# A graph network with two nucleus searches: one VectorE pass fewer in each search, logits placed between products, ScalarE passes reordered, three repair depths

## What is computed

```python
def _adj_from_feats(Xa, W1, W2, W3):
    logits = (Xa @ W1) @ W2 @ (Xa @ W3).T
    idx = argsort(-logits); vals = take(logits, idx)
    csum = cumsum(softmax(vals))
    k_i = sum(csum < 0.9) + 1          # keep the k_i largest of each row
    masked = where(rank < k_i, logits, -inf)
    return softmax(masked, axis=1)

h = relu(layernorm(x));  x = x + (A @ (h @ W + b)) / deg
h = relu(layernorm(x));  S = adj + I
Xf = Xb = Xa = h;  Z = 0
for s in range(2):
    A  = _adj_from_feats(Xa, W1, W2, W3)
    Xf = Rf @ Xf;  Xb = Rb @ Xb;  Xa = A @ Xa     # Rf, Rb: S over its row / column sums
    Z += Xf @ U1[s] + Xb @ U2[s] + Xa @ U3[s]
out = x + layernorm(h + Z) * gamma + beta
```

## Time and profile before

| | us |
|---|---|
| median of 3 runs | 2577.81 (2575.78 to 2578.23) |
| the profiled execution | 2577.75, of which the span of the trace 2576.0 |
| first step, from the first tile's last pass to the last tile's | 414.9 to 1294.3 |
| second step, the same | 1396.9 to 2514.2 |

### The profile page before, as it was taken

One profiled execution on the slowest core, in us unless ns is written; L12 is line 12 of the kernel. 1 busy time (PEld: TensorE's weight loads), 2 busy tenths in 40 slices (PEclk: granted clock), 3 DMA queues, 4 the chain that ended last, 5 costly groups with the idle time before them and its releaser, 6 DMA issues. The chain is left out here.

```text
span 2576.0 us, 33332 instructions
## 1 busy us (share of the span) xinstructions
PE 2014.6 (78%) x9898; PEld 1339.5 (52%) x9898; DVE 2227.2 (86%) x6888; ACT 1680.0 (65%) x1780; POOL 962.6 (37%) x1282
## 2 busy tenths in 40 slices
PE   2999465888888888888855887888888788888883
PEld 1555223566556665556633555555655555565552
DVE  6777658899889988889849999999999999999996
ACT  4334156788778877788636776777677677767730
POOL 1000042444434444344414354444535444453524
PEclk9999787999999999999976888888888888888896
DMA  6777210111111110111042000101010010101013
GB/s 226 286 284 271 92 44 17 47 45 36 41 43 47 47 45 31 42 47 46 32 156 80 19 19 19 38 19 38 19 38 19 22 35 19 37 20 37 18 61 121
DMA packets 65717, 167.54 MB, mean 65 GB/s; under 512 B 7037, under 2 KB 45307, under 8 KB 61947
## 3 DMA queue, kind: packets, MB, share of 16 engines
q1 hardware_dynamic: 65530, 165.43, 18.6%
HBM read 117.95 MB, written 47.45 MB: 64 GB/s over the span
## 5 line engine op out<-in xcount | busy, mean ns | idle before, releaser
L1348 PE MATMUL banks<-xa,pt 128*128 128x256 f32 x2704 | 660.2, 399 | 84.7 <-ACT pt L917 84.7
L893 ACT ACTIVATE junk_a<-pb_all,minus_t 128x3327 f16<-128x3327 f32 x151 | 463.5, 3069 | 261.5 <-POOLq L823 261.4
L1348 PEld LDWEIGHTS banks<-xa,pt 128*128 128x128 f32 x2704 | 527.8, 201 | 177.7 <-ACT pt L917 106.1
L1392 PE MATMUL banks<-region,at 128*128 128x512 f16 x2028 | 468.0, 392 | 0.0
L898 ACT ACTIVATE junk_a<-pb_all,minus_t 128x3327 f16<-128x3327 f32 x151 | 463.2, 3068 | 2.8
L1312 PE MATMUL banks<-keys,qs 64*128 64x512 f32 (+1 forms) x832 | 217.4, 642 | 221.8 <-DVE pb_all L1210 182.0
L808 POOL TENSOR_SCALAR over<-over,points 128x1 f32<-128x1 f32 x151 | 57.4, 380 | 821.7 <-ACT junk_a L898 821.6
L917 ACT ACTIVATE pt<-banks 128x896 f32<-128x896 f32 x208 | 178.0, 857 | 240.4 <-PE banks L1340 240.4
L1392 PEld LDWEIGHTS banks<-region,at 128*128 128x128 f16 x2028 | 205.8, 102 | 245.3 <-issue 28.7
L1312 PEld LDWEIGHTS banks<-keys,qs 64*128 64x128 f32 x832 | 83.6, 222 | 360.8 <-DVE pb_all L1210 264.5
L1210 DVE TENSOR_SCALAR_CACHE_REDUCE pb_all<-banks 128x1024 f32<-128x1024 f32 x260 | 208.9, 848 | 62.1 <-PE banks L1312 59.9
(11 more groups left out here) (225 smaller groups left out, 3309.2 us busy)
## 6 DMA issues: line engine op xcount, KB each, us to landing
at<-adjT_d SPq DMA_DIRECT2D x52, 832.0 KB, 4.9
region<-in_adj_dram SPq DMA_DIRECT2D x25, 1663.5 KB, 8.0
adjT_d<-at SPq DMA_DIRECT2D x26, 832.0 KB, 3.9
fb_d<-fb_sb SPq DMA_DIRECT2D x26, 256.0 KB, 2.0
region<-fb_d SPq DMA_DIRECT2D x2, 3328.0 KB, 19.2
y_d<-y_sb SPq DMA_DIRECT2D x50, 128.0 KB, 1.7
x_d<-pb_all SPq DMA_DIRECT2D x1, 3328.0 KB, 10.4
qs<-q_d SPq DMA_DIRECT2D x104, 32.0 KB, 4.2
```

Source lines behind the costliest of these rows:

```text
L893: nc.scalar.activation(junk_a[:, 0:w], pb[u][:, 0:w], ACT.Relu, scale=sign, bias=t, accum_out=over[u][:, 0:1])\
L1348: last = nc.tensor.matmul(bank[4][:, 0:D], pt[sl][:, t * P:(t + 1) * P], xa[:, t0 + t, :], start=(t0 + t == 0), stop=(t0 + t == T - 1))
L1392: last = nc.tensor.matmul(bank[5 + n][:, :], at[i.slot][:, t, :], mov, start=(t == 0), stop=(t == T - 1))
```

## The change

- Constants: the first step's search has one bisection fewer on DVE (BISECTIONS 5 to 4) and sorts 24 values, not 32; the second step's has a third rough level on ACT and POOL (ROUGH 2 to 3), one verifying pass fewer (VERIFIED 2 to 1) and sorts 40 values, not 64. The cut is now interpolated in both steps, with an aim of its own.
- In the second step DVE subtracts the whole of `below`; POOL's half and the semaphores `below_late` and `kept_late` are gone.
- PE makes the first two logits chunks of tile m ahead of the third and fourth product, and only the rest behind them.
- ACT's passes stand in a table STEPS: two copies come ahead of the first pass of tile j, the last pass stands behind the `zt` copies. In the second step the passes of tile m's first and second rough level stand as before around the copies of `sx`, with the second in the middle of them, and a third level ends the body, ahead of the next body's first copy.
- In the first step POOL makes `fb` in place of ACT, behind its levels.
- A repair has three depths (4, 24, all rounds), and PE counts flags three times a tile.

```diff
-    ROUGH = (0, 2)
-    BISECTIONS = (5, 3)
+    ROUGH = (0, 3)
+    BISECTIONS = (4, 3)
     ACT_BISECTIONS = (3, 3)
-    EARLY_BISECTIONS = (0, 2)
-    AIM = (12.0, 12.0)
-    VERIFIED = (0, 2)
+    EARLY_BISECTIONS = (0, 3)
+    AIM = (6.0, 16.0)
+    CUT_AIM = (6.0, 24.0)
+    VERIFIED = (0, 1)
     SEGMENTS = (8, 16)
-    SORTED = (32, 64)
+    SORTED = (24, 40)
     WSUB = (N + 1) // 4
-    MARGIN = 0.65
+    MARGIN = 0.45
...
-    LATE_SEGMENTS = SEGMENTS[1] // 2
-    LATE = LATE_SEGMENTS * ((N + 1) // SEGMENTS[1])
-    FEW_ROUNDS = 8
+    FEW_ROUNDS = 4
+    MORE_ROUNDS = 24
     ALL_ROUNDS = -(-N // 8)
-    LOOKS = 2
+    LOOKS = 3
...
-                        pool.wait_ge(S2("fb_hi")[k.slot], 3 * (k.use + 1))
+                        pool.wait_ge(S2("xfb")[k.slot], 2 * (k.use + 1))
+                        pool.wait_ge(S2("fb_stored")[1 - k.slot], 16 * (k + 1).use)
+                        ch.add(nc.gpsimd.tensor_copy(fb_sb[:, 0:D], xf_sb[k.slot][:, :]))
+                        ch.link(nc.gpsimd.tensor_scalar(xk_sb[:, :], xb_sb[k.slot][:, :], kappa[:, :], None, ALU.mult))
+                        ch.link(nc.gpsimd.tensor_copy(fb_sb[:, 2 * D:3 * D], xk_sb[:, :]))
                         nc.gpsimd.tensor_tensor(fb_sb[:, D:2 * D], xf_sb[k.slot][:, :], fb_sb[:, 0:D], ALU.subtract)\
                             .then_inc(S2("fb_lo")[k.slot], 1)
                         nc.gpsimd.tensor_tensor(fb_sb[:, 3 * D:4 * D], xk_sb[:, :], fb_sb[:, 2 * D:3 * D], ALU.subtract)\
                             .then_inc(S2("fb_lo")[k.slot], 1)
-                    if not first and i.inside(T):
-                        pool.wait_ge(S("below_late"), i.t + 1)
-                        late = pb[i.third][:, LATE:N]
-                        nc.gpsimd.tensor_tensor(late, late, below[:, LATE:N], ALU.subtract).then_inc(S("kept_late"), 1)
                     if not first:
                         level(m, 1)
+                        level(m, 2)
...
+                STEPS = ((), (0,), (1,), (2, 3), (4,), (5,)) if first else ((), (6,), (7,), (8, 9), (10,), (11,))
...
-                        if (0 if first else 1) <= c < NT - 1 and j.inside(T):
-                            sums(j, 2 * EARLY + c - (0 if first else 1))
-                    if j.inside(T):
-                        for n in range(3, 4) if first else range(6, 8):
-                            sums(j, n)
+                        if j.inside(T):
+                            for n in STEPS[c]:
+                                sums(j, n)
...
-                        for n in range(4, 6) if first else range(8, 10):
+                        for n in STEPS[NT]:
                             sums(j, n)
-                    if m.inside(T):
-                        exponentials(m)
...
+                    if j.inside(T):
+                        for n in STEPS[NT + 1]:
+                            sums(j, n)
+                    if m.inside(T):
+                        exponentials(m)
...
-                    if first and k.inside(T):
-
-                        fb = fb_sb
-                        act.wait_ge(S2("xfb")[k.slot], 2 * (k.use + 1))
-                        act.wait_ge(S2("fb_stored")[1 - k.slot], 16 * (k + 1).use)
-                        nc.scalar.activation(fb[:, 0:D], xf_sb[k.slot][:, :], ACT.Copy).then_inc(S2("fb_hi")[k.slot], 1)
-                        act.wait_ge(S2("fb_lo")[1 - k.slot], 2 * (k + 1).use)
-                        nc.scalar.activation(xk_sb[:, :], xb_sb[k.slot][:, :], ACT.Copy, scale=kappa[:, :]).then_inc(S2("fb_hi")[k.slot], 1)
-                        act.wait_ge(S2("fb_hi")[k.slot], 3 * k.use + 2)
-                        nc.scalar.activation(fb[:, 2 * D:3 * D], xk_sb[:, :], ACT.Copy).then_inc(S2("fb_hi")[k.slot], 1)
+                                if n == 0 and m.inside(T):
+                                    for q in range(2, 4):
+                                        sums(m, q)
+                    elif not first and m.inside(T):
+                        for q in range(2, 4):
+                            sums(m, q)
                     if not first and m.inside(T):
-                        for n in range(2, 4):
+                        for n in range(4, 6):
...
-                    cut = hi_t
-                    if not VERIFIED[s]:
-                        towards(cur[:, 0:1])
-                        cut = cur[:, 0:1]
+                    towards(cur[:, 0:1], CUT_AIM[s])
+                    cut = cur[:, 0:1]
...
-                        for g in [*range(LATE_SEGMENTS, G), *range(LATE_SEGMENTS)]:
+                        for g in range(G):
                             d = below[:, g * W8:(g + 1) * W8]
-                            ins = nc.vector.match_replace(d, rank[:, 8 * g:8 * g + 8], d, 0.0)
-                            if g == G - 1:
-                                ins.then_inc(S("below_late"), 1)
-                            elif g < LATE_SEGMENTS:
-                                ch.add(ins)
+                            ch.add(nc.vector.match_replace(d, rank[:, 8 * g:8 * g + 8], d, 0.0))
                         answer(i, 1)
                         ch.all_done()
-                        ch.add(nc.vector.tensor_tensor(p[:, 0:LATE], p[:, 0:LATE], below[:, 0:LATE], ALU.subtract))
+                        ch.add(nc.vector.tensor_tensor(p, p, below[:, 0:N], ALU.subtract))
...
-                            with dve.Fori(0, ALL_ROUNDS) as g:
-                                a_round(Chain(dve, "step_settle_3", base=TAKE * ALL_ROUNDS * i.n + TAKE * g), tg)
+                            with dve.Fori(0, MORE_ROUNDS) as g:
+                                a_round(Chain(dve, "step_settle_3", base=TAKE * MORE_ROUNDS * i.n + TAKE * g), tg)
+                            dve.sem_inc(S("unsettled"), 1)
+                            answer(i, 3)
+                            with dve.If(look(i, 3) > 0):
+                                with dve.Fori(0, ALL_ROUNDS) as g:
+                                    a_round(Chain(dve, "step_settle_4", base=TAKE * ALL_ROUNDS * i.n + TAKE * g), tg)
+                            with dve.Else():
+                                dve.sem_inc(S("settle_4"), TAKE * ALL_ROUNDS)
                         with dve.Else():
-                            dve.sem_inc(S("settle_3"), TAKE * ALL_ROUNDS)
+                            dve.sem_inc(S("any_un"), 1)
+                            dve.sem_inc(S("settle_3"), TAKE * MORE_ROUNDS)
+                            dve.sem_inc(S("settle_4"), TAKE * ALL_ROUNDS)
+                            dve.sem_inc(S("unsettled"), 1)
...
+                        count_flags(k, 2)
...
-                            if c == 1 and not first:
-                                pe.wait_ge(S("kept_late"), k.t + 1)
...
+                            if c >= 2 and m.inside(T):
+                                logits(m, c - 2, c - 1)
                             product(c)
                     if m.inside(T):
-                        logits(m)
+                        logits(m, 2 if k.inside(T) else 0, len(LCH))
```

20 lines of the change are left out of this document (8 added, 12 removed).

## The result

The changed kernel takes 2495.58 us (median of 4 runs, 2493.01 to 2497.49) against 2577.85 for the kernel before in the same session: ratio 0.969, 95% interval 0.967 to 0.971. The forecast was 2494. That the sum came out is not yet proof of its terms, and two of them are off in opposite directions, as the stretches show. They are cut at the same places as the earlier trace rows: first step, between the steps, second step; the columns are length, busy time of PE, PE's weight loads, DVE, ACT and POOL, then PE's granted clock and DMA.

What follows compares the result with a forecast made beforehand. DVE, 96% busy, was taken to bound the second step and to lead the first, where no engine is full. 2577.75 - 92 (first step) + 8 (second step) = 2494 us, range 2440 to 2545.

Steps and rivals of the forecast that it cites:

- First step, -92 forecast: First step: DVE loses 5.0 us a tile, PE decides next; period 35.2 to about 31.7 us, gain 92 us.
- ACT's chain: Second step: ACT's passes and waits for POOL's replies run to 29.1 us after DVE's subtraction ends; period taken as 45.2.
- E: Second step: the end of DVE's subtraction in a tile, from which ACT is followed; the next one comes 44.7 us later.
- The first question: Second step: ACT's request for POOL's reply to the first rough level, asked about 2 us before DVE's subtraction ends.
- the low clock: Second step: PE's clock at 0.50 after some 9 us idle before the products; up to 0.7 us a tile left over.
- The second step, +8 forecast: Second step: period 45.2 against 44.9, +8 us over 25 periods; what DVE sheds is lost in ACT's waits.
- the filling: Start of the second step: the extra rough level gives back the first tile's shorter search, 6.7 us.
- DVE's own work: Second step: removed pass, sort rounds and shorter lists sum to 6.7 us a tile, leaving DVE 38.2.
- That DVE stays the bound: Rival, second step: DVE still decides, 38.2 us a tile, total 2318 us; chance 3%.
- That ACT's questions miss DVE's passes: Rival, second step: requests to POOL fall outside DVE's passes; period 40, 2364 us, or 2445 if one misses; together 13%.
- ACT's longer chain: Rival, second step: sx runs at low clock or a fourth reply is blocked; +2 us a tile, 2545 us; 12%.
- Repairs: Rival: rounding leaves rows open; two tiles at first depth or one at second (47 + 202 us), 2743 us; 5%.

Runs made afterwards that it cites:

- the run with the repairs: Changed kernel with the second step's aims lowered to 12 and 16 and 64 values sorted, so that some rows stay open; 7424.55 us (one run).
- the run with the rough level behind: Changed kernel with the second step's third rough level moved behind the next body's first two turned chunks; 2454.22 us, ratio 0.952.

## Why the prediction was right, and where not

**First step, -92 forecast, -109.3 measured** (104.1 and 5.2 at the first tile). The mechanism holds: DVE no longer leads, PE does, DVE waits for flags (68.5 us in the 25 tiles). PE's work was sized right: the forecast's terms are 29.8 + 0.1 of work and 1.3 + 0.6 + 0.9 of waits, 32.7, less 1.0 for the lower clock, and the measured work is 722.34 / 25 = 28.9 at a clock of 1.00. The mis-sized term is the waits: 1.1 for the chunk (28.4 us in the 25 tiles), 0.6 for xo (15.7), 0.2 for DVE's draining (5.2) and 0.1 more, 2.1 where 2.8 stood. That makes 31.0 where 31.7 stood (31.2 in the steady tiles). The runs add what the sum didn't say: the gain needs the shorter search and ACT's order at once. The shorter search without the order gives 1.5 us a tile (33.7 against 35.2), the order without the shorter search nothing (35.5), both together 4.2, of which fb's move carries 0.9. The logits' place carries nothing there.

**Second step, ACT's chain: right to half a microsecond for 22 us.** From E, forecast and trace:

| | forecast | measured |
|---|---|---|
| ACT goes on after reply 1 | 1.5 | 1.4 |
| after reply 2 | 7.6 | 7.2 |
| first turned chunk copied | 9.8 | 9.3 |
| after reply 3 | 13.4 | 13.0 |
| after reply 4 | 22.4 | 21.9 |
| xo ends | 29.1 | 28.6 |
| subtraction begins | 41.2 | 41.9 |
| subtraction ends | 44.7 | 45.5 (46.6 in each second tile) |

The first question is asked 3.2 us before E and not 2, which changes nothing, as its reply ends with the subtraction.

**The step that failed is the one behind it.** I let xo and the adjacency product decide the flags, and gave the low clock "up to 0.7" after ACT's cover. In the trace `sx` ends at 1921.64 + 11.39 = 1933.03, E + 40.4, and is not last. Last is DVE: it drains the third logits at 1920.94 and has 13.6 us of own work from there to its subtraction at 1934.56. PE's logits were late (end at E + 28.3, 27 forecast), since the product behind the gap of 8.41 us took 4.80 us and not 3.29. On that way ACT covers nothing. By the forecast's own numbers it was a close second, E + 27 + 13.6 = E + 40.6 against the 41.2 over xo, and I never priced it. In each second tile the product takes 5.92 us, 1.12 more, and the tile 1.1 more. Filling the gap with work took 1.5 us a tile off, twice the 0.7.

**The second step, +8 forecast, +28.7 measured.** In steady tiles the period went from 45.1 to 46.1 (means of 22), +23 us; the first interval from 45.3 to 52.8, +7.5; the last two, -2. Ahead of the step 5.0 us came back. So the filling gave back the first tile's saving and 2.5 more; that term was right in kind.

**DVE's own work** fell about as forecast: in the tile shown 45.5 less its waits for logits, 4.38, 2.95 and 0.84 us, leaves 37.4, where 38.2 stood. Those waits are 8 us rather than the 5 to 6 of the forecast.

**The rivals.** That DVE stays the bound: excluded by 78% against 96%. The Trainium skill's rule to optimise the engine with the highest occupancy first (Perfetto Trace Analysis, Identifying the Most-Contended Engine) would have given 2318; measured are 2495.6, and the fastest kernel here has an added wait on DVE. That ACT's questions miss DVE's passes: in the changed kernel they didn't, but its price, 2 us a tile for one of the three, was real. Making DVE wait for one reply gave 1.9 us a tile (45.8 to 44.0) and, with the order changed, 2.3 (44.3 to 42.1). In the run with the repairs the first question did miss in every second tile, with only 2.2 us of work added on DVE, and the mean of the tiles without a repair fell by 1.7. ACT's longer chain, by `sx` at the low clock and +2 us a tile: `sx` stayed at full clock (11.39 us, as in the earlier trace rows); a cost of nearly that size came on the first product instead. In the run with the rough level behind, it did fall, to 12.84 us. Repairs: none in the changed kernel; their price per tile was right within 5 us.

The total within 2 us of the forecast thus rests on luck as well: 17 us more from the first step, 5 from between, 21 less from the second.

## What to carry to other kernels

Where two engines lock each other out, ask when a short reply is asked for, not how long it takes: a pass of DVE that waits until the reply is through can be faster than one that starts at once. Before taking work off the busiest engine, follow the ring of waits with that engine's work removed, and put whatever other engines need ahead of a long wait on a slow reply. And price the stretch behind an idle gap of PE at its low clock, on the way that is last.
